# Output projection of an attention layer: from fp32 products to three products of rounded parts, one step later in each pair

## The chip, the cores and the metric

The kernel runs on one core of a Trainium2 chip. The core has five engines that run side by side and meet only at semaphores: TensorE (PE; its weight loads are PEld), VectorE (DVE), ScalarE (ACT), GpSimd (POOL) and SyncE (SP), which here only issues DMAs. Time is the device time of the core in microseconds (us), less is better.

## The reference, cut to what matters

```python
x = x + tanh(g_xattn) * xattn(layernorm(x), ctx)          # 8 batches of 512 rows, 256 wide
x = x + tanh(g_ffn) * ffn(layernorm(x))                   # 64 experts, 8 chosen a row, and a shared one
# xattn: 16 heads of 64; 512 queries, 1024 keys
q = (lat @ Wq)                                            # per head
k, v = split(ctx @ Wkv);  k = rope(k, cos, sin)
attn = softmax(clip(q k^T / 8, -11, 11))
out = (attn @ v) @ Wo + bo                                # Wo is 1024 x 256
```

The change touches the last line, `(attn @ v) @ Wo`.

## The kernel before, in words

The program has four stages: setup (weights are split into parts and stored to DRAM), attention, the end of the routing, and the experts. The attention stage goes over 8 batches, and in each over 8 pairs of heads; batches 2 to 7 are one loop body. A pair has 8 steps, `c` = 0 to 7, one for each tile of 128 keys. Every engine's program is written by a function `step(g, m, c, ...)`, and the order of the work on an engine is the order in which `step` (with `route` and `prepare` on VectorE) writes it out. Three pairs are under way at a time: in pair g the keys, queries and values of g are projected (`ps_k`, `ps_v`), the scores and the exponentials of pair g-1 are made, and the result of pair g-2 is normalised and projected ("tail").

A product in which both operands are split goes as three: high by high, high by low, low by high. "High" is a copy to type fp32r (a rounded fp32) made by ScalarE, "low" the difference to the original, subtracted by VectorE. The projections of q, k and v and the scores go this way. The product with `v`, the sum of denominators and the output product are plain fp32.

The tail of a pair, before: step 1, TensorE sums the denominators (`ps_y`, L976), for which VectorE's `e_sum` of step 0 must be done. Step 2, ScalarE takes the logarithm and its exponential, VectorE refines the reciprocal (L1289, L1291). Steps 3 and 4, GpSimd multiplies the halves `o_n` (L1135, L1141). Steps 4 and 6, TensorE multiplies each half by `wo` into `ps_y` (L1004). Steps 5 and 7, VectorE adds it to `x` (L1260). `ps_y` is one PSUM bank, shared by the denominators, both halves of the output and the router, so each must wait until the one before has been read. All engines have one queue in order.

Between these, VectorE does the sum of exponentials (`e_sum`, L1286, 128x1024 in each of seven steps), the rotation of k (L1270, L1271), the low parts of q (L1264) and k (L1276), and the routing of the batch before (`route`): in pairs 1 and 2 bias and statistics, in pairs 4 to 6 probabilities, groups and experts, in pair 7 the counting of blocks (L461 to L478), in the next pair 0 the slots (L487 to L543). TensorE's part of the routing (rows turned in pairs 2 and 3, L320; logits in pair 4, L340; ranks in pair 6, L444 to L450) stands in step 5. GpSimd clips the exponentials (L1139) and issues the scatter of rows.

The product of q waits in the same PSUM bank as the keys' second half, which is why TensorE waits in step 4 for q's low part:

```python
if project and c in (0, 4):
    ...
    else:
        pe.wait_ge(s_qlo, 2 + g)
```

Of the kernel before, what the change touches and what calls it, by code (L numbers as in the profile page):

```python
# [11 lines left out]
P = 128  # L12
# [556 lines left out]
def setup(nc, pers, rope, router, ins, wqk_dram, wv_dram):  # L569

    with ExitStack() as ctx:
# [119 lines left out]
        def _(dve):  # L691
            for n in range(5 * QUADS):
# [3 lines left out]
                last.then_inc(lo_done, 1)  # L696
            latents = [pers.x1[:, t] for t in range(NT)]
# [9 lines left out]
def attention(nc, pers, rope, ins, wqk_dram, wv_dram, xs_dram, slots_dram, gates_dram, router):  # L707


    with ExitStack() as ctx:  # L710
# [166 lines left out]
        def _(pe):  # L877
# [11 lines left out]
            def step(g, m, c, project, attend, b=None, p=None):  # L889
# [90 lines left out]
                if routed(b) and c == 5 and p in (2, 3, 4, 6):  # L980
                    pe.wait_ge(s_add, 2 + g * 2 + 1)
# [910 lines left out]
```

## Time and profile before

| | us |
|---|---|
| median of 3 runs (2549.09 to 2558.55) | 2553.73 |
| the profiled execution | 2553.1 |
| its span, first to last instruction | 2551.4 |
| TensorE busy in it | 2294.6 |
| VectorE busy | 2055.1 |
| GpSimd busy | 1734.6 |
| ScalarE busy | 1524.2 |

The span is what the profile's rows add up to; the profiled execution's time has 1.7 us around it. Attention takes from some 34 to some 1940 us of the span. The granted clock of TensorE is 0.968 in the mean.

### The profile page before, as it was taken

The page shows a single profiled execution, that of the slowest core. Times are in us where ns is not written, and L with a number is a line of the kernel's source. Part 1 is how long each engine was busy: PE and PEld are TensorE (multiplying, and loading weights), DVE is VectorE, ACT ScalarE, POOL GpSimd, SP SyncE. Part 2 cuts the span into 40 slices and gives each one's busy share as a digit, 9 for nine tenths or more (in the row PEclk, how much of TensorE's full clock was granted, in tenths as well). Part 3 has the DMA queues.
Part 4 walks back from the last instruction along what each step waited for, and adds up shares of the span by engine and source line. Part 5 has one row for each costly group of instructions (what it writes and reads, how often), then busy time and mean ns, then how long its engine had stood idle before and what let it go on. Part 6 is the DMA issues. An engine that isn't in the chain of part 4 may idle for free. (4 is left out here: it accounts for less than half of the span.)

```text
span 2551.4 us, 40379 instructions
## 1 busy us (share of the span) xinstructions
PE 2294.6 (90%) x11366; PEld 1273.0 (50%) x11366; DVE 2055.1 (81%) x3571; ACT 1524.2 (60%) x2556; POOL 1734.6 (68%) x1515
## 2 busy tenths in 40 slices
PE   3999999999999999998999999999986989999980
PEld 2444445444444444344444444444443668987770
DVE  4778688978988897889789888978886759688884
ACT  4667666656666666666566666665662334766660
POOL 2767676588859876976788498759874700177776
PEclk9999999999999999999999999999997999999995
DMA  9533433111111112111112111111114428799994
GB/s 345 200 104 130 163 118 120 38 60 57 61 48 58 46 55 68 58 58 49 56 46 72 39 68 44 58 47 62 55 44 149 162 93 289 256 324 320 326 321 132
DMA packets 163585, 306.30 MB, mean 120 GB/s; under 512 B 19779, under 2 KB 99587, under 8 KB 160643
## 3 DMA queue, kind: packets, MB, share of 16 engines
q1 hardware_dynamic: 135234, 235.93, 27.1%
q0 software_dynamic: 24576, 67.14, 8.0%
q8 instruction: 107, 1.75, 0.3%
q14 instruction: 148, 1.20, 0.1%
q10 hardware_dynamic: 3520, 0.27, 0.1%
HBM read 173.51 MB, written 129.76 MB: 119 GB/s over the span
## 5 line engine op out<-in xcount | busy, mean ns | idle before, releaser
L1139 POOL TENSOR_SCALAR e<-e 128x1024 f32<-128x1024 f32 x512 | 689.8, 1347 | 357.5 <-ACT e L1047 303.6
L1047 ACT ACTIVATE e<-scores 128x1024 f32<-128x1024 f32 x512 | 525.1, 1026 | 410.9 <-PE scores L903 398.2
L1286 DVE TENSOR_TENSOR e_sum<-e_sum,e 128x1024 f32<-128x1024 f32 x384 | 585.7, 1525 | 160.7 <-POOL e L1139 151.9
L968 PE MATMUL ps_o<-e,v 128*64 128x512 f32 x2048 | 560.8, 626 | 7.0 <-POOL e L1139 6.6
L903 PE MATMUL scores<-q_t,k_t 64*128 64x512 f32 x3072 | 499.9, 431 | 4.7 <-issue 4.7
L903 PEld LDWEIGHTS scores<-q_t,k_t 64*128 64x128 f32 x3072 | 251.4, 186 | 365.2 <-issue 293.2
L1839 POOL DMA_INDIRECT more<-results_in_blocks,index x256 | 248.2, 970 | 256.9 <-DMA results_in_blocks<-more 175.2
L1065 ACT ACTIVATE k_sw<-ps_k 32x512 f32<-32x512 f32 x512 | 301.7, 589 | 89.8 <-PE ps_k L944 84.8
L1119 POOL DMA_INDIRECT rows_in_blocks<-room,a_r_index_now x192 | 267.7, 1394 | 49.0 <-issue 46.2
L944 PE MATMUL ps_k<-ctx_t,wqk 128*128 128x512 f32 x768 | 219.4, 422 | 34.1 <-DVE q_t L1264 34.1
L1131 POOL TENSOR_TENSOR k_c<-k_c,k_sw 128x512 f32<-128x512 f32 x128 | 199.6, 1559 | 32.6 <-DVE k_sw L1271 29.1
L929 PE MATMUL ps_v<-wv,ctx_t 128*128 128x512 f32 x768 | 212.2, 411 | 2.4 <-ACT v L1058 2.4
L968 PEld LDWEIGHTS ps_o<-e,v 128*64 128x64 f32 x2048 | 102.7, 136 | 192.1 <-issue 161.1
L1758 PE MATMUL ps_out<-down_all,room 128*128 (+1 forms) x632 | 191.6, 385 | 4.8 <-DVE room L1814 3.5
L944 PEld LDWEIGHTS ps_k<-ctx_t,wqk 128*128 128x128 f32 x768 | 138.3, 193 | 101.9 <-DVE q_t L1264 43.9
L1004 PE MATMUL ps_y<-wo,o_n 128*128 128x256 f32 x512 | 154.6, 427 | 21.1 <-POOL o_n L1135 17.8
L1276 DVE TENSOR_TENSOR k_t<-k_c,k_t 128x512 fp32r<-128x512 f32 x128 | 127.2, 994 | 54.2 <-ACT k_t L1073 54.2
L929 PEld LDWEIGHTS ps_v<-wv,ctx_t 128*128 128x128 f32 x768 | 134.7, 188 | 72.0 <-issue 45.4
L1783 DVE SCALAR_TENSOR_TENSOR x<-more,gate,x 128x256 f32<-128x256 f32 x256 | 123.0, 480 | 59.0 <-DMA more<-results_in_blocks,index 57.7
L1004 PEld LDWEIGHTS ps_y<-wo,o_n 128*128 128x128 f32 x512 | 92.1, 200 | 138.4 <-issue 94.8
L1734 PE MATMUL ps_hid<-x_nat,room 128*128 128x128 f32 x1024 | 156.5, 275 | 2.0 <-DVE room L1810 1.2
L1717 ACT ACTIVATE x_nat<-ps_x 128x256 f32<-128x256 f32 x320 | 121.1, 379 | 55.5 <-PE ps_x L1765 52.1
(288 smaller groups left out, 3511.4 us busy)
## 6 DMA issues: line engine op xcount, KB each, us to landing
rows_in_blocks<-room SPq DMA_DIRECT2D x16, 2560.0 KB, 10.4
x_nat<-rows_in_blocks SPq DMA_DIRECT2D x160, 256.0 KB
results_in_blocks<-more SPq DMA_DIRECT2D x80, 512.0 KB, 3.9
wqk<-wqk_pairs SPq DMA_DIRECT2D x65, 512.0 KB, 3.6
wv<-wv_quads SPq DMA_DIRECT2D x17, 1024.0 KB, 4.8
x_nat<-in_ctx SPq DMA_DIRECT2D x9, 1024.0 KB, 7.7
wo<-in_L_xattn_Wo SPq DMA_DIRECT2D x66, 128.0 KB, 3.6
down_all<-in_L_ffn_down_w SPq DMA_DIRECT2D x16, 512.0 KB, 7.1
```

The costliest lines, as they stand in the source:

```text
L903: mm = pe.matmul(scores[:, c % 2, hh * N:(hh + 1) * N], k_t[rows, att, kp, c * P:(c + 1) * P], q_t[rows, att, qp, :], start=(part == 0), s ...
L929: mm = pe.matmul(ps_v[:], ctx_t[:, a, cc, tile * P:(tile + 1) * P], wv[:, bb, cc], start=(k == 0), stop=(k == 5))
L944: mm = pe.matmul(ps_k[:], wqk[:, jj, bb, cc, 1], ctx_t[:, a, cc, half * N:(half + 1) * N], start=(k == 0), stop=(k == 5))
L968: mm = pe.matmul(ps_o[hh * DH:(hh + 1) * DH, :], v[:, tile, buf, hh * DH:(hh + 1) * DH], e[:, tile % 4, hh * N:(hh + 1) * N], start=(tile ...
L1004: mm = pe.matmul(ps_y[:, i, :], o_n[:, t * P:(t + 1) * P], wo[:, jj], start=True, stop=True)
L1047: act.activation(e[:, c % 4], scores[:, c % 2], ACT.Exp, scale=SCALE).then_inc(s_exp, 1)
L1065: st = act.activation(k_sw[to], ps_k[of], ACT.Copy)
L1119: pool.indirect_dma_start(xs_dram, bass.IndirectOffsetOnAxis(ap=router.index_now[:, t, k:k + 1], axis=0), router.rows[:, t], None).then_in ...
L1131: pool.tensor_tensor(k_c[:], k_c[:], k_sw[:], ALU.add).then_inc(s_turned, 1)
L1139: pool.tensor_scalar(e[:, c % 4], e[:, c % 4], EXP_HI, EXP_LO, ALU.min, ALU.max).then_inc(s_clip, 1)
L1286: dve.tensor_tensor(total, e[:, 0] if c == 2 else total, e[:, tile % 4], ALU.add).then_inc(s_sum, 1)
L1839: pool.indirect_dma_start(land[:, k], None, y_dram[0:blocks_of(b, k) * P, :], bass.IndirectOffsetOnAxis(ap=at, axis=0)).then_inc(y_in[k], 16)
```

## The change

`Wo` is loaded in setup, split into a high and a low part and stored to DRAM (`wo_dram`); each pair then loads both parts (256 KB in place of 128). In attention ScalarE copies each half of `o_n` to `o_hi` in steps 4 and 5, VectorE makes `o_lo`, and the output product becomes three fp32r products for each tile of 128 rows, in steps 5 and 7. The additions to `x` move to step 6 and to step 0 of the next pair, and TensorE's part of the routing to step 4. On VectorE the low part of q stands at the end of step 2, ahead of `route`, where it stood at the start of step 3, behind it.

```diff
-        OUT = {4: 0, 6: 1}
+        OUT = {5: 0, 7: 1}
...
+            act.wait_ge(wo_in, 16)
+            act.activation(split_o[:, :, 0], raw_o[:], ACT.Copy).then_inc(o_hi, 1)
...
+            dve.wait_ge(o_hi, 1)
+            dve.tensor_tensor(split_o[:, :, 1], raw_o[:], f32(split_o[:, :, 0]), ALU.subtract).then_inc(o_lo, 1)
...
-                if routed(b) and c == 5 and p in (2, 3, 4, 6):
-                    pe.wait_ge(s_add, 2 + g * 2 + 1)
+                if routed(b) and c == 4 and p in (2, 3, 4, 6):
+                    pe.wait_ge(s_rec, g + 1)
...
-                    pe.wait_ge(s_on, 2 + g * 2 + half + 1)
+                    pe.wait_ge(s_olo, g * 2 + half + 1)
...
-                        mm = pe.matmul(ps_y[:, i, :], o_n[:, t * P:(t + 1) * P], wo[:, jj], start=True, stop=True)
+                        for k, (part, w) in enumerate(((o_hi, 0), (o_hi, 1), (o_lo, 0))):
+                            mm = pe.matmul(ps_y[:, i, :], part[:, t * P:(t + 1) * P], wo[:, jj, w],
+                                           start=(k == 0), stop=(k == 2))
...
+                if c in (4, 5) and tail:
+                    half = c - 4
+                    part = slice(half * D, (half + 1) * D)
+                    if half == 0:
+                        act.wait_ge(s_out, 2 + g * 2)
+                    act.wait_ge(s_on, 2 + g * 2 + half + 1)
+                    act.activation(o_hi[:, part], o_n[:, part], ACT.Copy).then_inc(s_ohi, 1)
...
-                if (p, c) == (2, 4):
+                if (p, c) == (2, 3):
                     router.normalise(dve, 0)
...
-                if c - 1 in OUT and tail:
...
-                if project and c == 3:
-                    dve.wait_ge(s_qe, g + 1)
-                    dve.tensor_tensor(q_t[:, jj, 1], ps_k[:], f32(q_t[:, jj, 0]), ALU.subtract).then_inc(s_qlo, 1)
+                if c == 6 and tail:
+                    add_result(g, 0)
+                if c == 0 and exists(g - 3):
+                    add_result(g - 1, 1)
...
+                if project and c == 2:
+                    dve.wait_ge(s_qe, g + 1)
+                    dve.tensor_tensor(q_t[:, jj, 1], ps_k[:], f32(q_t[:, jj, 0]), ALU.subtract).then_inc(s_qlo, 1)
+                if c in (4, 5) and tail:
+                    half = c - 4
+                    part = slice(half * D, (half + 1) * D)
+                    dve.wait_ge(s_ohi, g * 2 + half + 1)
+                    dve.tensor_tensor(o_lo[:, part], o_n[:, part], f32(o_hi[:, part]), ALU.subtract).then_inc(s_olo, 1)
```

How the order changes on VectorE in pair 7 of the loop, from the refined reciprocal in step 2 to the sum of exponentials in step 4 (`q_t` is q's low part, `a_r_opened` the counting of blocks, `lat_t` and `k_t` low parts). Before:

```order
L1291 SCALAR_TENSOR_TENSOR r_den<-o_n,r_den 128x512
L273 REGISTER_ALU
L478 TENSOR_TENSOR a_r_opened<-a_r_opened 128x64
...
L1264 TENSOR_TENSOR q_t<-ps_k,q_t 128x512
...
L1286 TENSOR_TENSOR e_sum<-e_sum,e 128x1024
L1162 REGISTER_ALU
L1163 TENSOR_TENSOR lat_t<-affine,lat_t 128x512
L1276 TENSOR_TENSOR k_t<-k_c,k_t 128x512
```

With the change (line numbers are those of the changed kernel):

```order
L1318 SCALAR_TENSOR_TENSOR r_den<-o_n,r_den 128x512
L1322 TENSOR_TENSOR q_t<-ps_k,q_t 128x512
L273 REGISTER_ALU
L478 TENSOR_TENSOR a_r_opened<-a_r_opened 128x64
...
L1313 TENSOR_TENSOR e_sum<-e_sum,e 128x1024
L1189 TENSOR_TENSOR lat_t<-affine,lat_t 128x512
L1303 TENSOR_TENSOR k_t<-k_c,k_t 128x512
...
L1327 TENSOR_TENSOR o_lo<-o_n,o_hi 128x256
```

The low part of q passes the three rows of `a_r_opened`, and `o_lo` stands behind the `e_sum` of step 4.

How it changes on TensorE in pair 6, from the keys' second half in step 4 to the scores of step 6 (`scores` opens each step; L444 to L450 are the ranks). Before:

```order
L944 MATMUL ps_k<-ctx_t,wqk 128x512 x6
L968 MATMUL ps_o<-e,v 64x512 x2
L997 REGISTER_ALU
L1004 MATMUL ps_y<-wo,o_n 128x256 x2
L894 REGISTER_ALU
L903 MATMUL scores<-q_t,k_t 128x512 x6
...
L444 MATMUL ps_y<-a_r_taken,room 128x256
...
L450 MATMUL ps_y<-a_r_taken,room 128x64 x4
```

With the change:

```order
L959 MATMUL ps_k<-ctx_t,wqk 128x512 x6
L983 MATMUL ps_o<-e,v 64x512 x2
L444 MATMUL ps_y<-a_r_taken,room 128x256
...
L450 MATMUL ps_y<-a_r_taken,room 128x64 x4
L909 REGISTER_ALU
L918 MATMUL scores<-q_t,k_t 128x512 x6
...
L1020 MATMUL ps_y<-wo,o_hi 128x256 x2
L1020 MATMUL ps_y<-wo,o_lo 128x256
```

The ranks have moved ahead of the scores of step 5, and the output product behind them, to the end of step 5, as twice three products.

## Rows read from the trace of the kernel before

**Rows 1.** The page: the span, and busy time, share and instructions of each engine.

```profile
span 2551.4 us, 40379 instructions
PE 2294.6 (90%) x11366; PEld 1273.0 (50%) x11366; DVE 2055.1 (81%) x3571; ACT 1524.2 (60%) x2556; POOL 1734.6 (68%) x1515
```

**Rows 2.** Windows of batch 4: pairs 0, 2, 5, 7, sum of eight; first row: columns.

```profile
core 0: us, PE busy (x) PEld busy (x) DVE busy (x) ACT busy (x) POOL busy (x), PEclk, DMA share, GB/s
962.64:995.97 33.33, 31.03 (x140) 15.45 (x140) 27.87 (x54) 20.98 (x31) 19.02 (x14) 1.00 0.14 47
...
1024.16:1054.38 30.22, 25.56 (x114) 11.17 (x114) 25.05 (x39) 16.60 (x23) 27.81 (x26) 0.94 0.13 45
...
1112.34:1140.65 28.31, 27.83 (x130) 13.40 (x129) 27.87 (x47) 17.81 (x25) 21.72 (x19) 1.00 0.24 84
...
1167.77:1198.59 30.82, 26.73 (x137) 12.66 (x135) 29.02 (x33) 22.51 (x32) 14.66 (x13) 1.00 0.15 49
sum 235.95, PE 221.31 PEld 106.23 DVE 203.53 ACT 151.74 POOL 183.41; mean PE 27.66 PEld 13.28 DVE 25.44 ACT 18.97 POOL 22.93
```

**Rows 3.** Waits, 400 to 1800 us: who for whom, us in total, times, longest.

```profile
PE ps_k L944 <- DVE q_t L1264: 30.9, 18, 2.7
...
PE ps_y L1004 <- POOL o_n L1135: 11.1, 6, 1.9
```

**Rows 4.** Timeline of VectorE: start, duration, instruction, idle time before it.

```profile
1069.17 1.23 DVE L1286 TENSOR_TENSOR e_sum<-e_sum,e 128x1024 f32<-128x1024 f32 x1 [1.02 <-POOL e L1139]
...
1103.82 0.69 DVE L1276 TENSOR_TENSOR k_t<-k_c,k_t 128x512 fp32r<-128x512 f32 x1 [2.16 <-ACT k_t L1073]
...
1134.96 3.19 DVE L1286 TENSOR_TENSOR e_sum<-e_sum,e 128x1024 f32<-128x1024 f32 x2
...
1156.48 1.23 DVE L1286 TENSOR_TENSOR e_sum<-e_sum,e 128x1024 f32<-128x1024 f32 x1 [1.03 <-POOL e L1139]
...
1203.54 0.81 DVE L1291 SCALAR_TENSOR_TENSOR r_den<-o_n,r_den 128x512 f32<-128x512 f32 x1
...
1207.27 0.68 DVE L1264 TENSOR_TENSOR q_t<-ps_k,q_t 128x512 fp32r<-128x512 f32 x1
...
1210.38 1.21 DVE L1286 TENSOR_TENSOR e_sum<-e_sum,e 128x1024 f32<-128x1024 f32 x1
```

**Rows 5.** Timeline of TensorE: sums of denominators of pairs 4, 6, 0; pair 0's products.

```profile
1077.55 1.08 PE L976 MATMUL ps_y<-e_sum,ones_dh 128*64 128x512 f32 x4 [0.70 <-DVE e_sum L1286]
...
1138.79 1.03 PE L976 MATMUL ps_y<-e_sum,ones_dh 128*64 128x512 f32 x4
...
1196.34 1.08 PE L976 MATMUL ps_y<-e_sum,ones_dh 128*64 128x512 f32 x4 [0.54 <-DVE e_sum L1286]
...
1208.00 1.65 PE L944 MATMUL ps_k<-ctx_t,wqk 128*128 128x512 f32 x6 [2.18 <-DVE q_t L1264]
1209.58 1.08 PE L968 MATMUL ps_o<-e,v 128*64 128x512 f32 x4
1210.59 1.13 PE L1004 MATMUL ps_y<-wo,o_n 128*128 128x256 f32 x4
1211.65 0.96 PE L903 MATMUL scores<-q_t,k_t 64*128 64x512 f32 x6
```

**Rows 6.** Groups, 400 to 1800 us: busy us, mean ns of one, idle before.

```profile
L1141 POOL TENSOR_TENSOR o_n<-o_raw,r_den 128x256 f32<-128x256 f32 x47 | 69.9, 1488 | 3.8
...
L1260 DVE SCALAR_TENSOR_TENSOR x<-ps_y,minus_gate,x 128x512 f32 x88 | 65.2, 741 | 9.7 <-PE ps_y L1004 9.7
...
L1135 POOL TENSOR_TENSOR o_n<-o_raw,r_den 128x256 f32<-128x256 f32 x47 | 35.9, 763 | 28.1 <-DVE r_den L1291 25.9
...
L407 DVE TENSOR_TENSOR a_r_cmp_a<-a_r_cmp_a,a_r_cmp_b 128x256 f32<-128x256 f32 x6 | 2.5, 412 | 0.0
```

**Rows 7.** Setup, 0 to 34 us: groups of the weights' split, and the window.

```profile
L695 DVE TENSOR_TENSOR w_split_qk<-w_raw,w_split_qk 128x256 fp32r<-128x256 f32 x16 | 6.7, 489 | 13.7 <-ACT w_split_qk L646 13.7
L646 ACT ACTIVATE w_split_qk<-w_raw 128x256 fp32r<-128x256 f32 x16 | 5.1, 400 | 0.0
...
0.00:34.00 34.00, 4.31 (x18) 3.42 (x18) 18.46 (x58) 10.68 (x27) 12.73 (x26) 1.00 0.93 338
```

More of the change, by code:

```diff
@@ L566, in new_of, with setup @@
     return router.opened[:, 0, E_R:]
-def setup(nc, pers, rope, router, ins, wqk_dram, wv_dram):
+def setup(nc, pers, rope, router, ins, wqk_dram, wv_dram, wo_dram):
     with ExitStack() as ctx:
@@ L580, in setup @@
         split_v = sb("w_split_v", [P, QUADS, 2, C2, 4, P], FR)
+        raw_o = sb("wo_raw", [P, PAIRS, D])
+        split_o = sb("wo_split", [P, PAIRS, 2, D], FR)
+        wo_in, o_hi, o_lo, o_stored = sem("wo_in"), sem("wo_hi"), sem("wo_lo"), sem("wo_stored")
         natural = sb("rope_natural", [P, 2, ST, DH // 2])
@@ L624, in _ @@
                                  ).then_inc(stored, 16)
+            sp.wait_ge(o_lo, 1)
+            sp.dma_start(wo_dram.rearrange("g p n -> p g n"), f32(split_o[:]).rearrange("p g a n -> p g (a n)")
+                         ).then_inc(o_stored, 16)
+            sp.wait_ge(o_stored, 16)
             sp.wait_ge(stored, 16 * 5 * QUADS)
@@ L704, in _, with attention @@
             norms.normalise(dve, places[NT:], places[NT:], NT, 1)
-def attention(nc, pers, rope, ins, wqk_dram, wv_dram, xs_dram, slots_dram, gates_dram, router):
+def attention(nc, pers, rope, ins, wqk_dram, wv_dram, wo_dram, xs_dram, slots_dram, gates_dram, router):
     with ExitStack() as ctx:
@@ L733, in attention @@
         o_n = sb("o_n", [P, N])
+        o_hi = sb("o_hi", [P, N], FR)
+        o_lo = sb("o_lo", [P, N], FR)
         x_nat = pers.x_nat
@@ L1098, in _ @@
                 pool.sem_inc(skipped, 6)
+            for skipped in (s_ohi, s_olo):
+                pool.sem_inc(skipped, 4)
             for counted in (norms.normed, s_affine, s_cos, s_turned, s_vp, s_v, s_qlo):
@@ L1203, in _, with add_result @@
             numbered = [None]
+            def add_result(g, half):
+                dve.wait_ge(s_out, 2 + g * 2 + half + 1)
+                batch = ((g + 6) // PAIRS + B - 1) % B
+                rows = (pers.x1[:, batch * NT + 2 * half:batch * NT + 2 * half + 2, :] if isinstance(g, int) else
+                        pers.x1[:, bass.ds(batch * NT + 2 * half, 2), :]).rearrange("p a n -> p (a n)")
+                dve.scalar_tensor_tensor(out=rows, in0=y_flat, scalar=minus_gate[:], in1=rows,
+                                         op0=ALU.mult, op1=ALU.add).then_inc(s_add, 1)
             def route(b, p, c, g):
@@ L1301, in _ @@
             loop(dve, step, prepare=prepare)
+            add_result(B * PAIRS + 1, 1)
 def four_blocks(dram, i):
@@ L1868, in program @@
             rope = Rope(nc, tables)
-            setup(nc, pers, rope, router, ins, wqk_dram, wv_dram)
-            attention(nc, pers, rope, ins, wqk_dram, wv_dram, xs_dram, slots_dram, gates_dram, router)
+            setup(nc, pers, rope, router, ins, wqk_dram, wv_dram, wo_dram)
+            attention(nc, pers, rope, ins, wqk_dram, wv_dram, wo_dram, xs_dram, slots_dram, gates_dram, router)
         kept.more = ctx.enter_context(nc.sbuf_tensor("more", [P, MORE], F32))
```

32 lines of the change are left out of this document (14 added, 18 removed).

## The prediction

> **What bounds the kernel now.** I read the page's busy times first: TensorE is busy for 2294.6 of 2551.4 us and VectorE for 2055.1 [rows 1]. That names TensorE as the bound, but an average over stages can't say which wait ends last, so I went to the attention stage, which holds the change, and to one turn of its loop over batches (batch 4, 962.6 to 1198.6 us), pair by pair. The windows show two kinds of pairs [rows 2]. Pair 0 takes 33.33 us with VectorE busy for 27.87. Pair 5 takes 28.31 us with VectorE busy for 27.87, pair 7 takes 30.82 us with VectorE busy for 29.02: there VectorE has nothing to spare, because the routing of the batch before is done in those pairs. Pair 2 has neither full; it waits, and its granted clock is 0.94.
>
> Then the list of waits over 48 pairs (400 to 1800 us) [rows 3]: TensorE stands still for 30.9 us before the keys' second half (`ps_k` L944) until VectorE has written the low part of q; 11.1 us before the output product until GpSimd has `o_n`.
>
> Last, the timeline of VectorE, to see where its stretches without idle time begin and end [rows 4]. In pair 3 it runs from 1069.17 us on without a gap and TensorE's sum of denominators (L976) waits for it, 0.70 us. In pairs 4 to 6 it runs without a gap from 1103.82, and the sum at 1138.79 comes without a wait, 0.7 us after the `e_sum` that it needs. From 1156.48 (pair 6, step 6) it runs, but for the loop's branch, until the sum of the next pair 0 at 1196.34, which waits 0.54 us [rows 4, 5]. In these stretches VectorE sets the time, and whatever is added to it there is added to the kernel. In pair 0 it is TensorE that is held up: 2.18 us until q's low part at 1208.00, and then it is full for the rest of the pair while VectorE idles [rows 4, 5].
>
> **The change part by part.** *The products.* A half of the output product was two fp32 products of 256 columns, four instructions; from its start to the next instruction's is 1.06 us (1210.59 to 1211.65) [rows 5]. It becomes six fp32r products of 256 columns. The nearest row is the key projection, six fp32r products of 512 columns in 1.58 us, 0.263 us each [rows 5]; the fp32 instruction of 256 columns also takes 0.265 us, so two passes over 256 columns cost what one over 512 does. One pass over 256 columns must lie between half of that (0.13) and all of it (0.263); TensorE at its full clock of 2.4 GHz moves 256 columns in 0.107 us, and what the row of 512 has beyond its columns is 0.05. I take 0.16, so 0.96 us a half: 0.2 us less a pair. The bounds are 0.8 and 1.58 us a half. The Trainium skill ("TensorE: Matmul & The Clock Gate", section "LDWEIGHTS (loading the stationary operand)") has a load of 128 columns take P / 1.2 ns, 107 ns; in full ahead of each product that would give 0.21 us and 1.28 us a half, dearer than before. By that rule the row of 512 columns would be 0.32 us, and it is 0.263 [rows 5], so the trace shows half of the load hidden.
>
> *The splits.* ScalarE copies each half of `o_n` (128x256) to `o_hi`, VectorE subtracts. In setup the same two shapes cost 400 ns and 489 ns, pipeline included [rows 7]. ScalarE is busy for 22.51 of 30.82 us in the worst pair [rows 2], and `o_hi` stands in steps 4 and 5 where it waits for scores anyway: nothing. For VectorE the price is two subtractions a pair, 0.42 us each where nothing disturbs: L407, a subtraction's twin (two SBUF inputs, 128x256) at the very place in pair 5 where the first one will stand, has a mean of 412 ns [rows 6]. Where GpSimd works beside it, more: L1141 and L1135 are the same GpSimd operation on the two halves of `o_n`, and the one that meets `e_sum` takes 1488 ns and the other 763 [rows 6]; so 0.7 us can come on top. I take 0.42 to 1.1 each. The Trainium skill ("SBUF — State Buffer", section "Who interferes with whom") says that a VectorE operation with two SBUF inputs and a GpSimd one that reads SBUF exclude each other for a whole instruction. The rows of `o_n` agree with it; it is the rule that speaks against this change, since both new subtractions have two SBUF inputs.
>
> *The additions to x.* The addition of half 0 moves from the start of step 5 to the start of step 6, that of half 1 from step 7 to step 0 of the next pair, 0.74 us each [rows 6]. Counted over VectorE's stretches, from 1156.48 (pair 6, step 6) to the denominators of pair 0 there were three additions and are now four; one more stands also in the stretch from pair 4's step 7 to pair 6's denominators and in that of pair 3 from its step 6: +0.74 us in each.
>
> *q's low part ahead of the routing.* It moves from the start of step 3 to the end of step 2, ahead of the routing done there. In pair 0 `r_den` is ready at 1203.54 + 0.81 = 1204.35, so q's low part ends at about 1205.0 in place of 1207.95, and TensorE, which is there at 1205.8, waits for nothing: -2.2 us. In pair 7 it would come 2 us earlier as well, but this pair ends when VectorE ends, and its order alone doesn't shorten that: the wait reappears at the output product, for `o_lo`, or at the denominators.
>
> *The router's steps on TensorE* go from step 5 to step 4 and no longer wait for an addition. In pair 6 this takes away the wait of L444, but the product behind it waits for `o_lo`, which follows `e_sum` of step 4 by 0.42 where the addition followed it by 0.74; nothing of it survives, since VectorE is the bound from step 6 on. In pair 2 the output product waited for `o_n`; a step later it waits for `o_lo` after `e_sum`, and the turn of rows in step 4 waits for the normalised rows. I put pair 2 at +0.5.
>
> *Setup.* 1 MB of Wo is loaded, split and 2 MB stored. VectorE does one subtraction of 128x2048 more: twice the 1.21 us of 1024 columns is 2.4 [rows 4], eight times 6.7 / 16 us is 3.4 [rows 7]. The queues moved 338 GB/s over the first 34 us with the DMA engines 93% busy [rows 7]; 3 MB at 420 GB/s (its full slices) to 338 are 7.5 to 9 us, of which the lull before the barrier (the last 3 us) and gaps take some. The stage ends with the stores: +4.4 us, bounds 2.4 and 9. *End.* The two pairs after the loop are chains, and get a copy, a subtraction and an addition behind them, and two subtractions where TensorE waits for VectorE: +2.5.
>
> **The sum**, against where TensorE stands now, for one of the six batches 2 to 7: pair 0 -2.2 (wait) +0.4 (`o_lo` is ready at 1210.38 + 1.21 + 0.42 = 1212.0, TensorE is there at 1211.9, plus contention) -0.2 = -2.0; pairs 1 and 4 -0.2 each; pair 2 +0.5; pair 3 +0.42 +0.42 +0.74 = +1.6; pair 5 +0.84 +0.74 less 0.7 of slack = +0.9; pair 6 from step 6 and pair 7: 0.74 + 0.35 (partly in a gap of 1.03) + two subtractions of 0.42 to 1.1, +2.4. Together +3.0. Pair 0 also pays for a lower clock after its stall in some batches, as pair 2 does by its 0.94 [rows 2] (12% of 30.2 us at 1.2 GHz, 1.8 us lost); taking 0.6 us of that back leaves +2.4. Six batches +14.4, batches 0 and 1 -0.5, setup +4.4, end +2.5: +20.8 us. The profiled execution took 2553.1 us, 0.6 under the median, so about 2574 us. With the lower bounds everywhere (1.2 a batch, setup 2.4) it is +11, with the upper (4.8, setup 9) +39: 2564 to 2592.
>
> **Rivals.** *The waits that vanish are worth more than the added work* (0.24, faster). For it: VectorE idles 32 us a batch, 235.95 less 203.53 [rows 2], so the 7 us of `o_lo` have room; the waits for q (30.9 us in six batches) are the largest of TensorE's on VectorE. Against it: the room isn't in pairs 3, 5 and 7. If the stretches have slack that the timeline hides, pair 0 gives 2.0, pair 6 1.5, pair 2 0.5 with 1.8 of clock, pair 7 1.0 and the products 1.0 a batch: some 6 to 7, 38 us, less setup and end 7: 2523 us; half of it 2538. It decides where pair 7 gets no longer than 30.8 us.
>
> *The two cancel* (0.26, same): VectorE's stretches grow by 0.84 a pair without contention and half of the -2.2 is kept elsewhere too; then +0.4 a batch and setup: 2561 us.
>
> *VectorE's stretches grow* (0.42): my forecast, 2574 us.
>
> *The products are dearer* (0.08, slower): a short product may not cover the load of the next one's weights. Halfway between my 0.16 and the 0.263 of 512 columns [rows 5] a half takes 1.27 us, 0.62 a pair over my value; in the four pairs in which TensorE sets the time (0, 1, 4 and 6) that is 2.5 a batch, 17 us more in all: 2591 us. Against it stands that the row of 512 columns pays only 0.05 beyond its columns. The Trainium skill's rule on loads, above, points this way.
>
> Half a per cent (13 us) is about what a measurement of this kernel can tell from no change. Slower by more has the forecast and the dear products, 0.50; within it 0.26; faster 0.24. The range reaches down to the half-kept gain and up to the dear products: 2536 to 2594.
>
> **What the profile after would show.** Right: the wait of `ps_k` L944 on q is under 5 us in 48 pairs; TensorE waits for VectorE's `o_lo` or `e_sum` in pairs 2, 3 and 7 instead; VectorE's idle time falls by more than 7 us a batch; L1141's mean on GpSimd stays near 1.5 us or grows; pair 0 is near 31 us and pair 7 near 33; the attention stage starts 4 to 5 us later; a half of the output product is 0.96 us from start to start. Wrong: if pair 7 is no longer than before, the stretches were not the bound; if the clock is full in pairs 0 and 2 of every batch, I undervalued the stalls; if a half takes over 1.2 us, the loads were not hidden.

## The result and the profile after

The changed kernel takes 2548.43 us (median of 20 runs, 2545.48 to 2554.55), the kernel before 2554.03 on the same chip (20 runs): a ratio of 0.9981, with a 95% interval of 0.9973 to 0.9989. It is 5 us faster, within the half per cent. I had forecast 2574; 2548 lies within the range that I gave (2536 to 2594), but I had the direction wrong. The profiled execution took 2554.55 us, the longest of the 20; I don't read its span against that of before, but its stages.

The page of the kernel after, as [rows 1]:

```profile
span 2552.8 us, 41080 instructions
PE 2281.6 (89%) x11622; PEld 1297.4 (51%) x11622; DVE 2129.9 (83%) x3700; ACT 1570.2 (62%) x2685; POOL 1711.9 (67%) x1515
```

TensorE does 256 instructions more and is busy for 13 us less; VectorE is busy for 75 us more. The windows of batch 4 after, with the columns of [rows 2]; shown are pairs 0, 3, 5, 6 and 7 and the sum:

```profile
970.94:1001.59 30.65, 30.65 (x147) 15.72 (x145) 29.12 (x55) 20.43 (x31) 18.19 (x15) 1.00 0.21 69
...
1059.74:1085.66 25.92, 23.51 (x120) 10.78 (x118) 24.00 (x28) 17.64 (x27) 23.71 (x20) 1.00 0.17 57
...
1118.22:1145.70 27.48, 27.48 (x134) 13.60 (x132) 25.00 (x43) 18.40 (x27) 21.36 (x18) 1.00 0.27 92
1145.70:1172.73 27.03, 25.23 (x132) 12.49 (x131) 26.54 (x35) 17.52 (x25) 24.82 (x20) 1.00 0.16 55
1172.73:1205.72 32.99, 29.22 (x141) 14.24 (x139) 28.29 (x35) 23.67 (x35) 15.12 (x14) 0.90 0.14 45
sum 234.78, PE 222.43 PEld 110.10 DVE 210.96 ACT 156.29 POOL 179.12; mean PE 27.80 PEld 13.76 DVE 26.37 ACT 19.54 POOL 22.39
```

In pairs 0 and 5 TensorE is busy from the first to the last moment. Pair 5, which I had forecast to grow by 0.9 us, is shorter than before by 0.8 (28.31 in [rows 2]). The waits over 48 pairs, as [rows 3]:

```profile
PE ps_y L320 <- DVE rows_now L312: 18.7, 6, 3.1
PE ps_y L991 <- DVE e_sum L1313: 17.7, 16, 1.4
PE ps_y L1020 <- DVE o_lo L1327: 16.3, 7, 2.6
...
PE ps_k L959 <- DVE q_t L1322: 6.3, 11, 0.7
```

The wait for q's low part has gone from 30.9 to 6.3 us, and two new ones stand there: for the normalised rows in pair 2 (3.1 in each batch, step 4) and for `o_lo` (up to 2.6, in pair 7).

Setup, from the timeline of all engines: the split of Wo, the store of its parts, the first instructions of the next stage:

```profile
22.82 1.91 ACT L656 ACTIVATE wo_split<-wo_raw 128x2048 fp32r<-128x2048 f32 x1 [2.57 <-DMA wo_raw<-in_L_xattn_Wo]
...
24.77 2.29 DVE L708 TENSOR_TENSOR wo_split<-wo_raw,wo_split 128x2048 fp32r<-128x2048 f32 x1 [1.36 <-ACT wo_split L656]
...
27.09 0.37 SPq L631 DMA_DIRECT2D wo_pairs<-wo_split  x1
...
43.13 0.32 SPq L842 DMA_DIRECT2D wqk<-wqk_pairs  x1
...
44.71 1.09 PE L896 MATMUL ps_v<-ident,x_nat 128*128 128x128 f32 x4 [20.90 <-POOLq L1126]
```

The store is issued at 27.09 and the stage ends 16 us later; attention's first product is at 44.71, where it was at 35.53, the start of the same product before. That is 9.2 us, and I had put 4.4.

### The profile page after: what moved, and what is told of

It is laid out like the page before. It is cut to its first block and busy times, and to the rows that moved or that the text cites. A ratio compares the mean times of both kernels' runs of the same rounds, so it can differ in the third digit from the quotient of the medians.

```text
span 2552.8 us, 41080 instructions
## 1 busy us (share of the span) xinstructions
PE 2281.6 (89%) x11622; PEld 1297.4 (51%) x11622; DVE 2129.9 (83%) x3700; ACT 1570.2 (62%) x2685; POOL 1711.9 (67%) x1515
## 3 DMA queue, kind: packets, MB, share of 16 engines
q1 hardware_dynamic: 137314, 247.73, 28.4%
## 5 line engine op out<-in xcount | busy, mean ns | idle before, releaser
L1313 DVE TENSOR_TENSOR e_sum<-e_sum,e 128x1024 f32<-128x1024 f32 x384 | 597.5, 1556 | 72.7 <-POOL e L1165 72.4
L918 PE MATMUL scores<-q_t,k_t 64*128 64x512 f32 x3072 | 508.2, 437 | 9.9 <-issue 8.1
L1082 ACT ACTIVATE k_sw<-ps_k 32x512 f32<-32x512 f32 x512 | 301.3, 589 | 64.4 <-PE ps_k L959 59.6
L1145 POOL DMA_INDIRECT rows_in_blocks<-room,a_r_index_now x192 | 246.1, 1282 | 49.0 <-issue 48.0
L959 PEld LDWEIGHTS ps_k<-ctx_t,wqk 128*128 128x128 f32 x768 | 138.0, 193 | 74.7 <-issue 35.6
L1020 PEld LDWEIGHTS ps_y<-wo,o_hi 128*128 128x128 f32 x512 | 82.3, 200 | 152.6 <-issue 88.8
L1327 DVE TENSOR_TENSOR o_lo<-o_n,o_hi 128x256 fp32r<-128x256 f32 x128 | 108.5, 847 | 54.6 <-ACT o_hi L1093 54.6
L1020 PE MATMUL ps_y<-wo,o_hi 128*128 128x256 f32 x512 | 115.8, 320 | 42.6 <-DVE o_lo L1327 30.3
```

Of the source, the lines that this page charges most:

```text
L918: mm = pe.matmul(scores[:, c % 2, hh * N:(hh + 1) * N], k_t[rows, att, kp, c * P:(c + 1) * P], q_t[rows, att, qp, :], start=(part == 0), s ...
L959: mm = pe.matmul(ps_k[:], wqk[:, jj, bb, cc, 1], ctx_t[:, a, cc, half * N:(half + 1) * N], start=(k == 0), stop=(k == 5))
L1082: st = act.activation(k_sw[to], ps_k[of], ACT.Copy)
L1145: pool.indirect_dma_start(xs_dram, bass.IndirectOffsetOnAxis(ap=router.index_now[:, t, k:k + 1], axis=0), router.rows[:, t], None).then_in ...
L1313: dve.tensor_tensor(total, e[:, 0] if c == 2 else total, e[:, tile % 4], ALU.add).then_inc(s_sum, 1)
```

## The experiments

Three theories. A: each part of the change has a price of its own, and the prices add up. B: an earlier q only moves a wait. C: VectorE has more slack than A gives it, so that an earlier q is all gain and work added to it is free. Letters used in one expectation only are explained in it. "Change" below is the difference of the medians of a kernel and of the kernel before on the same chip. The first four ran on one chip (before: 2550.58), the next four on another (2552.06), the last three on a third (2699.39; below).

| kernel | us | ratio, 95% | change |
|---|---|---|---|
| after (result) | 2548.43 | 0.9981 (0.9973 to 0.9989) | -5.6 |
| setup_alone | 2562.43 | 1.0042 (1.0027 to 1.0058) | +11.8 |
| qlo_alone | 2526.68 | 0.9906 (0.9888 to 0.9925) | -23.9 |
| steps_alone | 2521.41 | 0.9873 (0.9851 to 0.9895) | -29.2 |
| wo_late | 2543.76 | 0.9965 (0.9951 to 0.9978) | -6.8 |
| after_qlo_back | 2564.18 | 1.0044 (1.0029 to 1.0059) | +12.1 |
| no_olo | 2493.91 | 0.9766 (0.9749 to 0.9782) | -58.2 |
| olo_more | 2566.68 | 1.0046 (1.0029 to 1.0064) | +14.6 |
| products_twice | 2625.87 | 1.0286 (1.0265 to 1.0307) | +73.8 |
| order_alone | 2672.60 | 0.9899 (0.9879 to 0.9919) | -26.8 |
| splits_unused | 2693.84 | 0.9978 (0.9963 to 0.9993) | -5.5 |
| after_again | 2695.55 | 0.9987 (0.9976 to 0.9999) | -3.8 |

The second table tells where in a batch each one differs. It is worked out from the timelines of TensorE: from the start of a pair's first product of q (L954 before) to that of the next pair's, mean of batches 2 to 6, in us.

| pair | 0 | 1 | 2 | 3 | 4 | 5 | 6 | 7 | sum |
|---|---|---|---|---|---|---|---|---|---|
| before | 33.7 | 28.3 | 30.2 | 25.1 | 32.9 | 28.3 | 27.1 | 32.1 | 237.8 |
| setup_alone | 33.8 | 28.3 | 30.1 | 25.1 | 32.9 | 28.3 | 27.1 | 31.6 | 237.2 |
| qlo_alone | 30.9 | 28.4 | 30.2 | 25.1 | 32.9 | 27.8 | 27.1 | 31.4 | 233.7 |
| order_alone | 32.7 | 27.8 | 30.1 | 25.8 | 32.9 | 28.0 | 26.1 | 31.7 | 235.0 |
| steps_alone | 30.9 | 27.8 | 30.2 | 25.9 | 32.9 | 27.8 | 26.1 | 32.0 | 233.5 |
| splits_unused | 31.2 | 27.8 | 30.7 | 26.2 | 32.9 | 27.8 | 27.4 | 34.6 | 238.5 |
| after | 30.9 | 27.5 | 30.7 | 25.9 | 32.6 | 27.5 | 27.0 | 34.5 | 236.5 |
| after_again | 31.2 | 27.5 | 30.7 | 25.9 | 32.6 | 27.5 | 27.0 | 33.5 | 235.8 |
| wo_late | 30.9 | 27.5 | 30.7 | 25.9 | 32.6 | 27.5 | 27.0 | 34.4 | 236.5 |
| after_qlo_back | 31.9 | 27.5 | 30.7 | 25.9 | 32.6 | 27.7 | 27.0 | 35.6 | 238.9 |
| no_olo | 30.2 | 27.0 | 30.2 | 25.0 | 32.1 | 27.0 | 25.9 | 32.0 | 229.3 |
| olo_more | 32.1 | 27.7 | 30.9 | 26.3 | 32.6 | 27.5 | 27.4 | 33.7 | 238.1 |
| products_twice | 32.1 | 29.0 | 31.0 | 27.5 | 34.0 | 28.9 | 27.3 | 37.3 | 247.0 |

Batch 4, from which the forecast was made, is not typical in pair 7: it takes 30.82 us there at a granted clock of 1.00, the other four batches of the kernel before 32.2 to 32.8 at 0.95. In pair 0 it is the reverse: batches 2 and 6 have 0.95 and 34.9 us, the other three 1.00 and 32.1 to 33.4.

**setup_alone**: the kernel before with Wo's split and store in setup, which nothing reads.

```diff
+            act.activation(split_o[:, :, 0], raw_o[:], ACT.Copy).then_inc(o_hi, 1)
+            dve.tensor_tensor(split_o[:, :, 1], raw_o[:], f32(split_o[:, :, 0]), ALU.subtract).then_inc(o_lo, 1)
+            sp.dma_start(wo_dram.rearrange("g p n -> p g n"), f32(split_o[:]).rearrange("p g a n -> p g (a n)")
+                         ).then_inc(o_stored, 16)
```

> The kernel before with only the new part of setup (Wo is loaded, split by ScalarE and VectorE, and both parts are stored), the attention stage as it was. Theory A: the new transfers of 3 MB stand in the way of a stage that its DMAs bound, and attention starts later by as much as in the changed kernel, 9.2 us; nothing behind takes it back: about 2562 us, +9. Rival B (my forecast's value): the lull before the barrier hides half of it, +4.4. Rival C: the late start is hidden behind the loads of x that VectorE waits for in any case: +0 to +2.

Measured +11.8 (by the ratio +7 to +15): the price of the lengthened setup, over twice my term of 4.4. In its profile attention's first product comes 10.2 us later than before (45.69 against 35.53) and batch 2 begins 8.8 later (494.90 against 486.06), so nothing near it hides the late start; the last pair's q is only 4.4 us later (1885.91 against 1881.51), but this profiled execution, 2554.99 us, is the shortest of the six.

**qlo_alone**: the kernel before with q's low part at the end of VectorE's step 2.

```diff
-                if project and c == 3:
+                if project and c == 2:
```

> The kernel before with one edit: the low part of q at the end of step 2, ahead of the routing. Theory A: pair 0 loses its wait of 2.2 us and, where the clock fell after it, some 0.7 more; pair 5 loses 0.5; in pair 7 the wait only moves, since VectorE has no idle time there: -3 us in each of six batches, about 2535 us. Rival B: VectorE bounds all the pairs with routing, and the wait moves in pair 0 too: 2550 us or more. Rival C: all waits for q (5.2 us a batch) were lost time: about 2522 us.

Measured -23.9, the side of C. The windows of pairs 0 and 5 of its batch 4:

```profile
955.97:986.88 30.91, 30.91 (x142) 15.51 (x140) 26.04 (x52) 19.59 (x29) 17.41 (x14) 1.00 0.17 57
...
1103.17:1130.93 27.76, 27.76 (x130) 13.42 (x128) 27.32 (x47) 17.79 (x25) 21.45 (x19) 1.00 0.25 86
```

Pair 0 gives 2.8 us, pair 5 0.55, pair 7 0.7: 4.1 a batch, 24 in six. In pair 5 VectorE is still busy for 27.32 of 27.76 us, and yet the pair is shorter, because TensorE no longer stands.

**steps_alone**: the order of the change (products in steps 5 and 7, additions in 6 and 0, router, q's low part), with the plain fp32 products and no split anywhere.

```diff
-                    pe.wait_ge(s_olo, g * 2 + half + 1)
+                    pe.wait_ge(s_on, 2 + g * 2 + half + 1)
...
-                        for k, (part, w) in enumerate(((o_hi, 0), (o_hi, 1), (o_lo, 0))):
+                        mm = pe.matmul(ps_y[:, i, :], o_n[:, t * P:(t + 1) * P], wo[:, jj], start=True, stop=True)
```

(The diffs from here on are against the changed kernel, but for order_alone and splits_unused, which are against steps_alone.)

> The changed kernel's order (output products in steps 5 and 7, additions in step 6 and step 0, router's part in step 4, low part of q ahead of the routing), but with the plain fp32 products of before, no split of Wo and none of o_n. Theory A: the moves give and take about the same (the waits for o_n and for the additions go, the turn of rows in pair 2 waits 3 us for the normalised rows), so it comes out as with the low part of q alone, 2535 us within 5. Rival B: the additions that moved into VectorE's full stretches cost 0.74 us in each of three stretches: 2548 us.

Measured -29.2, so neither A (-15) nor B: beside the earlier q the order brings something of its own, which order_alone looks for. It is the fastest kernel here that computes all of the reference, 24 us under the changed one by the changes. Its pairs 3, 5, 6 and 7 of batch 4:

```profile
1038.26:1064.52 26.26, 23.99 (x116) 10.58 (x114) 21.56 (x26) 16.77 (x25) 24.13 (x19) 1.00 0.14 46
...
1097.39:1125.14 27.75, 27.75 (x130) 13.38 (x128) 26.27 (x49) 17.81 (x25) 21.99 (x18) 1.00 0.24 86
1125.14:1151.26 26.12, 25.45 (x129) 12.28 (x127) 22.80 (x28) 16.63 (x23) 23.99 (x19) 1.00 0.14 46
1151.26:1182.78 31.52, 27.75 (x137) 13.76 (x135) 27.55 (x32) 23.98 (x34) 19.15 (x15) 0.95 0.13 42
```

**wo_late**: the changed kernel with Wo split pair by pair in batch 0 (loaded raw, split in steps 6 and 7, stored for the later batches) in place of setup.

```diff
+                if isinstance(g, int) and 1 <= g <= PAIRS and c == 7:
+                    dve.wait_ge(s_whi, g)
+                    dve.tensor_tensor(wo[:, 1 - jj, 1], rows_now[:, 0], f32(wo[:, 1 - jj, 0]), ALU.subtract
+                                      ).then_inc(s_wlo, 1)
```

> The changed kernel, but Wo isn't split in setup: in batch 0 each pair loads 128 KB of Wo, ScalarE and VectorE split it in steps 6 and 7 (VectorE has idle time there), and the parts are stored for the later batches. Theory A (setup costs 9 us of time that nothing hides): 2539.5 us, 9 less than the changed kernel's 2548.4. Rival (the late start is hidden later): 2546 us or more.

Measured -6.8 to the kernel before, so 1 us under the changed kernel by the medians and 4 by the ratios. Its timeline has attention's first product at 35.94 again, 8.8 earlier; but batch 0 takes 209.7 us from q to q in place of 206.5, so the split has a price in batch 0 too. Behind that the start of batch 2 and the last output product are both 6.6 to 6.9 us earlier than in the profile of the changed kernel (1941.31 against 1947.94 for the latter). By the runs the gain is less than A's 9, but the two intervals (-12 to -6 here, -7 to -3 for the changed kernel) leave anything from 0 to 10: neither theory is excluded.

**after_qlo_back**: q's low part back in step 3.

```diff
+                if project and c == 3:
-                if project and c == 2:
```

> The changed kernel with one line moved back: q's low part again in VectorE's step 3, not at the end of its step 2. Theory A (TensorE's wait for q's low part is lost time whatever stands around it): the 24 us that this move alone gave in the kernel before come back, 48 x 0.5, so about 2572 us. Theory B (with o's low parts in steps 4 and 5 VectorE is late elsewhere in the pair, so that an earlier q only moves the wait): not over 2556 us.

Measured +12.1, so 18 over the changed kernel: nearer A (24) than B (under 8). By the table it is paid in pairs 0 (1.0), 5 (0.2) and 7 (1.1). The prices don't add up exactly; that with `o_lo` in the pair the wait is sometimes another's already is an argument and not shown.

**no_olo**: without the low part of o, which the output product leaves out.

```diff
-                        for k, (part, w) in enumerate(((o_hi, 0), (o_hi, 1), (o_lo, 0))):
+                        for k, (part, w) in enumerate(((o_hi, 0), (o_hi, 1))):
...
-                    dve.tensor_tensor(o_lo[:, part], o_n[:, part], f32(o_hi[:, part]), ALU.subtract).then_inc(s_olo, 1)
```

> The changed kernel without o's low part: VectorE makes no o_lo, and TensorE makes two products of the three for each tile and waits for o_hi instead (the kernel leaves out the low part of o in the output product). Two products of 256 columns a half at 0.115 us are 0.46 us a pair, 22 us in 48. By the runs so far the parts of o cost some 27 us in attention: the steps alone gave 2521, the setup adds 11, 48 x 2 x 0.15 = 14 us come off for the shorter products, and the change measured 2548. Theory A (they are VectorE's o_lo, 96 of 0.81 us, about a third of it on the path): 2548 - 22 - 27 = 2499 us. Theory C (they are ScalarE's o_hi and the shape of the chain, VectorE has slack in these steps): 2548 - 22 = 2526 us.

Measured -58.2, 53 under the changed kernel: A (49) holds, C (22) falls. Its pairs 5 to 7 of batch 4:

```profile
1090.26:1117.26 27.00, 27.00 (x130) 13.12 (x128) 26.64 (x41) 18.43 (x27) 22.41 (x19) 1.00 0.27 93
1117.26:1143.16 25.90, 24.74 (x129) 12.01 (x127) 24.98 (x35) 17.47 (x25) 23.77 (x19) 1.00 0.15 52
1143.16:1174.60 31.44, 27.19 (x136) 13.47 (x134) 27.59 (x32) 24.48 (x36) 18.81 (x15) 0.95 0.13 40
```

Pair 5 loses 0.48, the time of four products and nothing else, though VectorE lost two `o_lo` there; pair 3 loses 0.9, pair 6 1.1 and pair 7 1.5 to 2.5. So `o_lo` costs nothing in pair 5, and what it costs lies mostly in pairs 6 and 7, with 0.4 in pair 3.

**olo_more**: one subtraction of 128x256 more a pair, in step 4.

```diff
+                    if half == 0:
+                        dve.tensor_tensor(o_lo[:, D:2 * D], o_n[:, part], f32(o_hi[:, part]), ALU.subtract)
+                    else:
+                        dve.wait_ge(s_olo, g * 2 + 1)
```

> The changed kernel with one subtraction of 128x256 more on VectorE in step 4 of each pair: the second half's low part is already made there and made again in step 5. 48 x 0.81 = 39 us of VectorE's time more, nothing else. Theory A (each o_lo costs a third of its time): 2548 + 14 = 2562 us. Theory D (VectorE is the bound in these steps, all of it on the path): 2587 us. Theory C (slack there): within 3 us of 2548.

Measured +14.6, so 20 over the changed kernel, of some 39 us of VectorE's time added: between A (14) and D (39). Pairs 5 and 7 of batch 4:

```profile
1128.20:1155.68 27.48, 27.48 (x135) 13.59 (x133) 25.01 (x44) 18.42 (x27) 21.35 (x18) 1.00 0.27 92
...
1183.07:1217.88 34.81, 29.32 (x141) 14.15 (x139) 31.46 (x38) 24.97 (x37) 16.27 (x15) 0.90 0.12 37
```

Pair 5 takes 27.48 us as after, and VectorE is busy there for 25.01 as after (25.00), with one instruction more. Pair 7 is long in this batch, but its mean of 33.7 isn't above the changed kernel's (33.5 and 34.5); by the table the added work is paid in pair 0 (1.0), in pairs 3 and 6 (0.4 each) and in pairs 1 and 2 (0.2 each).

**products_twice**: six products for each tile in place of three, so that the output product comes out doubled.

```diff
-                        for k, (part, w) in enumerate(((o_hi, 0), (o_hi, 1), (o_lo, 0))):
+                        for k, (part, w) in enumerate(2 * ((o_hi, 0), (o_hi, 1), (o_lo, 0))):
```

> The changed kernel with the three output products of a tile issued twice (the output product comes out doubled): six products of 256 columns more for each half, 6 x 0.115 = 0.69 us, 1.38 us a pair, 66 us in 48. Theory T (TensorE's time is the path in nearly all of the pair): 2548 + 66 = 2614 us. Theory V (TensorE has some 3 us of waits for VectorE in a pair, which take up half of it): about 2580 us.

Measured +73.8, so 79 over the changed kernel: T (66), and more. Pair 5 of batch 4, and pair 3 of batches 3 and 4:

```profile
1158.88:1187.78 28.90, 28.90 (x147) 15.02 (x145) 26.38 (x51) 18.43 (x27) 20.23 (x18) 1.00 0.25 87
```

```profile
851.89:880.25 28.36, 26.21 (x133) 13.24 (x131) 23.61 (x27) 17.52 (x27) 24.95 (x20) 0.94 0.15 51
1098.83:1124.85 26.02, 24.77 (x133) 12.22 (x131) 24.16 (x28) 17.53 (x27) 23.72 (x20) 1.00 0.17 56
```

12 products more make 28.90 of 27.48: 0.118 us each. Of the pairs that wait, 2 and 6 take up nearly all of their part (+0.3 each). Pair 3 takes it up where the clock stays full (26.02 us, after 25.92) and pays 2.4 us more in the three of five batches in which the granted clock is 0.94. Pair 7 takes up nothing (+2.8), at 0.91 where it had 0.90: why it pays more than its products isn't shown.

**order_alone**: steps_alone with q's low part left in step 3.

```diff
+                if project and c == 3:
-                if project and c == 2:
```

> The kernel before with the steps of the change, but q's low part left in step 3: output products in steps 5 and 7, additions in 6 and 0, the router moved with them, plain products, nothing split. With q's low part moved too this gave 2521 (32 under before), and q's low part alone 24. Theory A (the two are independent, the moved additions and products bring 8 themselves): 2542 us, 0.997 of before. Theory Q (q's low part is all that helps, and the other steps only help behind it): 2550, no change. Theory R (the changed kernel with q's low part put back lost only 17): about 2537 us, 15 under before.

This chip is slower in all kernels, but not in attention: after_again's last product of attention's output ends at 1944 us of the span, where the profile of the result has 1948; then the experts' 400 us (2100 to 2500) have 226 GB/s of DMA where the other has 305. So I compare by differences. Measured -26.8: neither A nor Q, more than R. (The expectation's 32 and 8 take the kernel before from another chip; on steps_alone's own it is 29 and 5.) It reaches most of the gain without moving q: pairs 0 and 6 give 1.0 each, pair 1 0.6, pairs 5 and 7 0.3 and 0.4, and pair 3 takes 0.7. By the timelines attention's last output product comes 22.8 us earlier than before here, 24.0 in qlo_alone and 31.5 in steps_alone. That the additions to x, 0.74 us each, no longer stand ahead of what TensorE waits for is an argument and not shown. The two gains overlap: each alone is 23 to 27, both together 29 to 32.

**splits_unused**: steps_alone with `o_hi` and `o_lo` made and waited for, and not used.

```diff
-                    pe.wait_ge(s_on, 2 + g * 2 + half + 1)
+                    pe.wait_ge(s_olo, g * 2 + half + 1)
...
+                    act.activation(o_hi[:, part], o_n[:, part], ACT.Copy).then_inc(s_ohi, 1)
...
+                    dve.tensor_tensor(o_lo[:, part], o_n[:, part], f32(o_hi[:, part]), ALU.subtract).then_inc(s_olo, 1)
```

> The steps of the change with the parts of o made and not used: ScalarE makes o_hi, VectorE o_lo, TensorE waits for o_lo and then runs the two plain fp32 products of a half (1.06 us) of the kernel before; Wo is not split. Against the steps alone (2521) it has only the splits more, against the changed kernel (2548) only the plain products for the three, without the setup's split (11 us). By the run without o_lo the low parts cost some 31 us on VectorE and the high parts some 7. Theory A (these add up): 2521 + 38 = 2559 us. Theory C (the run without o_lo had two effects at once, the splits cost under 20): 2540 us. What the changed kernel's shorter products save comes out as this run + 11 - 2548: 14 if it is 0.15 us for each of 96 halves, near 40 if it is more.

Measured -5.5, so 24 over steps_alone, by the medians nearer C (under 20) than A (38). Its chip being another, 24 is the less sure number of the balance: in the profiled executions (6 and 3 us over their medians) the last pair's q comes 31 us later than in steps_alone (1883.89 against 1852.53), and no_olo has 30 for `o_lo` alone (53, less 23 for the products that it leaves out). So the price of the parts of o is 24 to 31. Pairs 5 to 7 of batch 4:

```profile
1112.68:1140.43 27.75, 27.75 (x130) 13.39 (x128) 25.26 (x48) 18.41 (x27) 20.82 (x18) 1.00 0.24 86
1140.43:1167.80 27.37, 25.49 (x128) 12.29 (x127) 24.54 (x30) 17.47 (x25) 25.16 (x20) 1.00 0.15 49
1167.80:1202.50 34.70, 29.60 (x137) 14.62 (x135) 31.21 (x36) 24.71 (x36) 15.89 (x14) 0.90 0.11 31
```

Against steps_alone pair 5 is the same (27.75), pair 6 has 1.25 us more, pair 7 3.2 in this batch and 2.6 in the mean.

**after_again**: the changed kernel once more.

> The changed kernel itself once more, for a profile nearer its median: 2548 us, and a span near 2547. Every theory expects the same.

Measured -3.8. Its pair 7 has a mean of 33.5 us, where the first profile has 34.5; the other seven agree within 0.3. So pair 7 varies by a microsecond between executions of one program, and by up to 3.8 between the batches of one (31.95 to 35.77), and nothing is built on less.

## Why the prediction was wrong

The balance, in us against the kernel before: the order and q's low part -29, the parts of o +24 to +31, setup +12, the shorter products -13 (pair 5 takes 27.48 us in place of steps_alone's 27.75, 0.27 in each of 48 pairs); that is -6 to +1, and the change measured -5.6 and -3.8. I had +20.8. By its steps:

**"In these stretches VectorE sets the time, and whatever is added to it there is added to the kernel."** This step failed, and it is the largest part of the miss. In pair 5 before, TensorE was busy for 27.83 of 28.31 us [rows 2]; the row stood in front of me, and I read VectorE's column beside it. The sum of denominators at 1138.79, at the end of the same stretch, came without a wait; I took that as 0.7 us of slack and no more. A stretch without a gap on VectorE isn't a stretch full of work. Its groups in pair 5 of batch 4, before (us busy, mean ns):

```profile
L1286 DVE TENSOR_TENSOR e_sum<-e_sum,e 128x1024 f32<-128x1024 f32 x6 | 9.5, 1582 | 0.1
L1276 DVE TENSOR_TENSOR k_t<-k_c,k_t 128x512 fp32r<-128x512 f32 x2 | 2.2, 1098 | 0.0
```

And after:

```profile
L1313 DVE TENSOR_TENSOR e_sum<-e_sum,e 128x1024 f32<-128x1024 f32 x6 | 7.6, 1272 | 0.0
...
L1327 DVE TENSOR_TENSOR o_lo<-o_n,o_hi 128x256 fp32r<-128x256 f32 x2 | 1.9, 964 | 2.1 <-ACT o_hi L1093 2.1
...
L1303 DVE TENSOR_TENSOR k_t<-k_c,k_t 128x512 fp32r<-128x512 f32 x2 | 1.4, 679 | 0.0
```

The same six sums and two subtractions take 2.7 us less; two `o_lo` are new, and VectorE idles for 2.1 before them. How long one instruction takes depends on what GpSimd does beside it. Four lines of the changed kernel, pairs 5, 6 and 7:

```profile
1133.48 1.38 POOL L1157 TENSOR_TENSOR k_c<-k_c,k_sw 128x512 f32<-128x512 f32 x1
1133.64 1.50 DVE L1327 TENSOR_TENSOR o_lo<-o_n,o_hi 128x256 fp32r<-128x256 f32 x1
...
1161.17 0.41 DVE L1327 TENSOR_TENSOR o_lo<-o_n,o_hi 128x256 fp32r<-128x256 f32 x1
...
1185.83 1.62 POOL L1165 TENSOR_SCALAR e<-e 128x1024 f32<-128x1024 f32 x1 [1.56 <-ACT e L1064]
```

The GpSimd instruction at 1133.48 ends at 1134.86 and the subtraction beside it at 1135.14, 0.28 us later; that at 1185.83 ends at 1187.45 and `o_lo` of 1186.48 (1.25 us, below) at 1187.73, 0.28 later again. Of the 94 `o_lo` that the trace has in 48 pairs, 49 take over 0.5 us, and every one of these ends 0.27 to 0.29 us after a GpSimd instruction that was running; the others take about 0.42. The `e_sum` of the kernel before does the same: each of the 96 that the timeline lists singly and over 1.26 us ends 1.06 to 1.09 us after a GpSimd instruction, and undisturbed it takes 1.21. So VectorE, which looked full from end to end, was waiting inside its instructions, and its busy time is no amount that stays. The two engines meet at more than semaphores here. no_olo and olo_more say the same as experiments: in pairs 4 and 5, and within 0.2 us in pair 1, the time goes with TensorE's instructions alone. There the forecast's +0.9 (pair 5) is -0.8, a miss of 1.7 us in each of six batches, 10 us.

**Pair 0** was right: -2.0 forecast with `o_lo` and -0.6 for the clock that comes back, measured -2.5 to -2.9, with the granted clock at 1.00 in all five batches where it had been 0.95 in two. **Pair 1**, -0.2 forecast, is -0.8. TensorE's waits there went whole. The 0.6 in pair 1 came with the order (order_alone has it, qlo_alone hasn't), and I hadn't priced it. **Pair 3**, +1.6 forecast, is +0.85: steps_alone has it already (25.9), so it is the moved addition, and `o_lo`, forecast at 0.84, adds 0.3 that the shorter products take back. It is the same step that failed, by half. **Pair 2**: +0.5 forecast, +0.45 measured. **Pair 4**: -0.2 and -0.3. Beside pair 5 these make some 1.6 us a batch, 9 to 10 us.

**Pairs 6 and 7**, +2.4 forecast, are +1.3 (after_again) and +2.3 (after) together: the mechanism is right, and it is the place where the parts of o are paid. The order takes 1.0 from pair 6, the splits give it back (splits_unused), and pair 7 grows by 2.6. Its timelines, VectorE and then TensorE, after:

```profile
1185.34 1.21 DVE L1313 TENSOR_TENSOR e_sum<-e_sum,e 128x1024 f32<-128x1024 f32 x1
1186.48 1.25 DVE L1327 TENSOR_TENSOR o_lo<-o_n,o_hi 128x256 fp32r<-128x256 f32 x1
```

```profile
1184.16 1.08 PE L983 MATMUL ps_o<-e,v 128*64 128x512 f32 x4
1187.78 0.80 PE L1020 MATMUL ps_y<-wo,o_hi 128*128 128x256 f32 x2 [2.55 <-DVE o_lo L1327]
```

TensorE is done at 1185.23 and stands for 2.55 us: `o_lo` is queued behind an `e_sum` of 1.21 and itself takes 1.25. In steps_alone the same product waits for nothing. Behind the stall the clock is at its lower level (1.2 GHz), from 1187.78 to 1193.89:

```profile
1187.78:1193.89 6.11, 6.11 (x20) 3.20 (x20) 6.11 (x8) 2.37 (x3) 3.41 (x2) 0.50 0.00 0
```

In these 6.11 us it runs a half of the output product, six scores, four `ps_v` and four `ps_o`, which take 0.91, 0.89, 0.58 and 1.01 us from start to start where the clock is full, 3.4 in all. So the lower clock costs 2.7 us there, as much as the stall. It is not all new: pair 7 has 0.95 in four of five batches before and 0.90 in all five after (31.95 us at 0.95 and 35.77 at 0.90 are the ends in after_again). The forecast had no term for it: pair 7 before was read from the one batch at 1.00.

**The price of `o_lo`**, 0.42 to 1.1 us: in 48 pairs it has a mean of 811 ns, 0.41 in pair 6 (1161.17) and 1.25 and 1.49 in pair 7:

```profile
L1327 DVE TENSOR_TENSOR o_lo<-o_n,o_hi 128x256 fp32r<-128x256 f32 x94 | 76.2, 811 | 30.8 <-ACT o_hi L1093 30.8
```

Of the 78 us that 96 of them take, some 30 are paid (no_olo: 53 less four products of 0.118 in 48 pairs, 23). By the rule of the Trainium skill ("SBUF — State Buffer", section "Who interferes with whom"), named in the prediction, such subtractions and GpSimd exclude each other; the 49 slow ones, each ending 0.28 us behind a GpSimd instruction, agree.

**The product**, 0.96 us a half forecast, 1.06 before. From pair 1 of batch 4 after:

```profile
1014.67 0.51 PE L1020 MATMUL ps_y<-wo,o_hi 128*128 128x256 f32 x2
1015.01 0.29 PE L1020 MATMUL ps_y<-wo,o_lo 128*128 128x256 f32 x1
1015.14 0.40 PE L1020 MATMUL ps_y<-wo,o_hi 128*128 128x256 f32 x2
1015.37 0.28 PE L1020 MATMUL ps_y<-wo,o_lo 128*128 128x256 f32 x1
1015.58 0.96 PE L918 MATMUL scores<-q_t,k_t 64*128 64x512 f32 x6
```

0.91 from start to start. products_twice has 0.118 us for a product that joins a group, so 0.2 of the half is paid once. The 0.263 of a 512-column product [rows 5], a sixth of 1.58, held that part too. The rule on weight loads of the Trainium skill ("TensorE: Matmul & The Clock Gate", section "LDWEIGHTS (loading the stationary operand)"), 107 ns in full ahead of each product, would have made it 0.21; the run shows that within a group hardly anything of it is paid: 0.118 is 0.011 over the 0.107 us that 256 columns take at 2.4 GHz.

**Setup**, +4.4 forecast, is +9.2 on the timeline and +11.8 in the run alone. I had worked out 7.5 to 9 us for 3 MB at the measured rate and then taken off a lull and gaps that the transfer would fill. Nothing came off: the stage ends with its DMAs, at 93% busy and some 340 GB/s in both kernels, and 3.1 MB by 340 is 9.2. The upper bound was the number. **The end**, +2.5 forecast: from the last pair's q to the last addition 66.6 us after, 64.4 before.

Together: 26 to 29 us less than my sum in batches 2 to 7 (from batch 2's first q to the last pair's 1395.5 us before, 1384.1 and 1380.8 after; by pairs it is 5, then 3 and 1, and batch 7, which the table's means leave out, has its share), 5 more in setup, 3 to 4 more in batches 0 and 1: 17 to 21 of the 26 us that I was off. The rest lies between single executions, as far as can be seen: the profiled ones of before and after stand 0.9 under and 6 over their medians of 2554.03 and 2548.43. The rival of vanished waits had the right mechanism and, with setup and pair 7 in it, the wrong size; it said itself what would decide, pair 7 at 30.8 or less, and pair 7 is at 33 to 35 (its mean before was 32.1, not 30.8). 2548 lies between its half-kept gain (2538) and the rival that the two cancel (2561).

What stays open: why olo_more costs half of its added time, and no more, isn't put down to single waits; why pair 7 pays more than its products in products_twice; and how much of setup's price wo_late saves, 1 to 4 us by the runs and 6.6 by the profiles.

## What to carry to other kernels

Before calling an engine the bound of a stretch, subtract the busy time of the other one from the stretch's length: 0.5 us of 28.3 was all that a faster VectorE could have won there. What added work costs that number doesn't tell; here two `o_lo` cost nothing, because VectorE had been waiting inside its instructions. Compare the mean of a form there with the same form elsewhere. Look at more than one batch, with the granted clock, before taking a pair's time as the one to beat. And split a change into its order and its work: here the order was worth 29 us, while the parts of o took at least 24 back and setup 12, for products that came out shorter by 13 in all.

## What the hardware showed that I hadn't expected

The output products in fp32r cost 0.118 us for 256 columns, with six loads of different weights in a row, and about 0.2 us once a group; before, two fp32 products of 256 columns took 1.06. One and the same subtraction of 128x256 on VectorE took from 0.41 to 1.49 us within 30 us of one batch, and each slow one ended 0.27 to 0.29 us after a GpSimd instruction that ran beside it. Behind a stall of 2.55 us TensorE ran at half its clock for 6.1 us. And a chip moved 226 GB/s in the experts' stage where another moved 305, with attention within 0.3% on both; why isn't shown.
